# Gate and projection stage: the load of the next sums moved up the DMA queue, and two maxima and one difference moved up VectorE's order

## What is computed

```
out = wave_attention(x)                                  # sampled sums, per token 256 channels
se  = sigmoid(silu(out @ w_se1 + b_se1) @ w_se2 + b_se2) # squeeze, excite
y   = layernorm(x + silu((out * se) @ w_out))
z   = layernorm(y) * ln1_w + ln1_b
q, k, v = split(z @ w_qkv)
y2  = y + softmax(q k^T / 4) v @ w_proj                   # attention, 16 heads
...                                                      # second norm, choice of one of 8 experts, norm
```

## Time and profile before

| | us |
|---|---|
| median of 3 runs | 1665.49 |
| lowest, highest | 1662.57, 1666.0 |
| the profiled execution | 1665.16 |
| its span in the trace | 1663.1 |
| PE busy (93%) | 1542.4 |
| DVE busy (80%) | 1329.3 |
| ACT busy (61%) | 1012.0 |
| busy PE in the gate and projection stage's slices | 8 to 9 tenths |

### The profile page before, as it was taken

The page is one execution under the profiler, slowest core; times in us unless marked ns, Lnnn a source line. Parts: engine busy times, 40 slices in busy tenths (PEclk is TensorE's granted clock), DMA queues, the critical chain, the costliest instruction groups (busy, mean ns, idle before and its releaser), DMA issues. The chain is left out here.

```text
span 1663.1 us, 29306 instructions
## 1 busy us (share of the span) xinstructions
PE 1542.4 (93%) x10078; PEld 838.7 (50%) x10078; DVE 1329.3 (80%) x3006; ACT 1012.0 (61%) x1745; POOL 197.3 (12%) x372
## 2 busy tenths in 40 slices
PE   7588998979988999999999999999998859999997
PEld 6465666655553222222222222222222859999996
DVE  5899999846778888898889888988880756777773
ACT  2699999935445777777777777777776532222221
POOL 3011111131110000000000000000000351222222
PEclk9899999999999999999999999999999978999999
DMA  3300110026956322222232222212302756666661
GB/s 107 89 8 14 49 44 20 22 88 204 264 178 188 77 50 63 71 69 46 61 71 71 52 59 71 71 43 61 70 21 84 237 209 225 208 209 204 204 204 57
DMA packets 159154, 172.22 MB, mean 104 GB/s; under 512 B 72912, under 2 KB 118992, under 8 KB 159008
## 3 DMA queue, kind: packets, MB, share of 16 engines
q1 hardware_dynamic: 153600, 156.60, 32.5%
q0 software_dynamic: 4432, 13.50, 2.1%
q10 hardware_dynamic: 976, 0.24, 0.1%
HBM read 120.73 MB, written 49.23 MB: 102 GB/s over the span
## 5 line engine op out<-in xcount | busy, mean ns | idle before, releaser
L1629 DVE TENSOR_REDUCE at_mx<-at_pmx 128x1 f32<-128x512 f32 x980 | 617.6, 681 | 56.3 <-PE at_pmx L1695 55.4
L1616 ACT ACTIVATE at_p<-at_pst 128x512 f32<-128x512 f32 x1024 | 532.7, 604 | 208.3 <-PE at_pst L1714 208.2
L1695 PE MATMUL at_pmx<-at_k,at_q 96*128 96x512 bf16 x980 | 373.8, 382 | 0.0
L1714 PE MATMUL at_pst<-at_q,at_k 99*128 99x512 bf16 x1024 | 345.7, 379 | 4.7 <-ACT at_p L1616 2.6
L1724 PE MATMUL at_pacc<-at_p,at_v 128*32 128x512 f32 x2048 | 272.7, 604 | 0.9 <-ACT at_p L1616 0.7
L1695 PEld LDWEIGHTS at_pmx<-at_k,at_q 96*128 96x128 bf16 x980 | 95.1, 97 | 238.7 <-DVE at_mx L1629 180.0
L1714 PEld LDWEIGHTS at_pst<-at_q,at_k 99*128 99x128 bf16 x1024 | 98.7, 97 | 156.0 <-ACT at_p L1616 92.8
L873 PE MATMUL ws_pA<-ident,ws_A 128*128 128x128 f32 x1088 | 149.9, 283 | 24.7 <-ACT ws_A L655 22.0
L2226 ACT ACTIVATE ex_hT<-ex_pH 128x1024 f32<-128x1024 f32 x39 | 39.9, 1024 | 204.7 <-PE ex_pH L2281 204.7
L873 PEld LDWEIGHTS ws_pA<-ident,ws_A 128*128 128x128 f32 x1088 | 119.8, 144 | 84.6 <-ACT ws_A L655 39.7
L2241 DVE STREAM_TRANSPOSE ex_zr<-ex_row 32x64 f32<-32x64 f32 x608 | 143.2, 236 | 17.0 <-DMA ex_row<-scratch_routed 8.4
(11 more groups left out here) (271 smaller groups left out, 1568.2 us busy)
## 6 DMA issues: line engine op xcount, KB each, us to landing
ex_w<-in_L_ffn_w SPq DMA_DIRECT2D x39, 1024.0 KB, 5.4
at_q<-scratch_qs SPq DMA_DIRECT2D x192, 64.0 KB, 2.8
at_k<-scratch_ks SPq DMA_DIRECT2D x192, 64.0 KB, 2.9
ex_row<-scratch_routed SPq DMA_DIRECT2D x39, 258.0 KB, 5.0
scratch_v<-gp_v SPq DMA_DIRECT2D x8, 1024.0 KB, 7.9
at_v<-scratch_v SPq DMA_DIRECT2D x32, 256.0 KB, 3.6
w<-in_L_ffn_w SPq DMA_DIRECT2D x16, 512.0 KB, 4.7
scratch_qs<-gp_split SPq DMA_DIRECT2D x16, 384.0 KB, 3.1
```

The lines of the kernel that those rows point to most:

```text
L1616: a.activation(pt[k // 2 % 4][:, k % 2, :], pst[bank(w, k)][:], ACT.Exp).then_inc(exped, 1)
L1629: v.reduce_max(mx[u % 2][:, m // 2, m % 2:m % 2 + 1], pmx[bank(w, m)][:], AX.X).then_inc(red, 1)
L1695: nc.tensor.matmul(pmx[bank(w, m)][:], qst[u][0:ROWS, h, nt * P:(nt + 1) * P], kst[u][0:ROWS, h, kh * HALF:(kh + 1) * HALF], start=True, s ...
L1714: nc.tensor.matmul(pst[bank(w, k)][:], kst[u][:, h, t * P:(t + 1) * P], qst[u][:, h, p * HALF:(p + 1) * HALF], start=True, stop=True).then ...
```

## The change

It has two parts. On SP's queue `load_sums(i + 2)` is issued behind `load_x(i + 1)` and ahead of `load_scores` and of the three stores of chunk i-1, where it stood behind them. On VectorE, after the normalised chunk (L1303), `peaks(i, 5, 6)` and `remain(prev, 2)` go ahead of `low(prev, 0)` and `low(prev, 1)`, and `peaks(i, 6, 7)` goes ahead of `gate_sums(i + 1)`. Nothing is added or removed.

```
 def chunk(i, prev):                       # SP
     if i + 1 < CHUNKS:
         load_x(i + 1)
+    if i + 2 < CHUNKS:
+        load_sums(i + 2)
     if FIRST - 1 <= i < FIRST - 1 + AHEAD:
         load_scores(i - (FIRST - 1))
     if prev is not None:
         for q in range(3):
             store_split(prev, q)
-    if i + 2 < CHUNKS:
-        load_sums(i + 2)
     sp.wait_ge(y0d, i * T + T)
...
                                           # VectorE
+    peaks(i, 5, 6)
     if prev is not None:
+        remain(prev, 2)
         low(prev, 0)
         low(prev, 1)
-        remain(prev, 2)
-    peaks(i, 5, 6)
+    peaks(i, 6, 7)
     if more:
         gate_sums(i + 1)
-    peaks(i, 6, 7)
     if prev is not None:
         remain(prev, 3)
```

## The result

The changed kernel takes 1656.8 us (median of 6 runs, 1655.49 to 1659.32), the kernel before, run beside it, 1666.61 (6 runs, 1662.57 to 1669.06). The ratio is 0.995 with a 95% interval of 0.9933 to 0.9966, that is 5.7 to 11.2 us less. The forecast was 1657.1 us, 8.1 less. The profiled execution took 1656.7 us, its span 1654.9.

A forecast was written before the change was run, and what follows sets the result against it. TensorE was taken to bound the stage, with VectorE near it in chunks with peaks. Gains of 0.6, 0.8, 1.0, 3.3 - 0.3, twice 1.4 and -0.1 sum to 8.1 us: 1665.2 - 8.1 = 1657.1 us, range 1654 to 1662.

The forecast's parts named there:

- chunk 1: TensorE's part 5 waits 0.27 us for the difference and pO 0.31 for the gate; 0.6 gained.
- chunk 2: The squeeze's lost time waiting for the sums' load goes, let through by the earlier gate: 0.8 us gained.
- chunk 3: The squeeze's lost time waiting for the sums' load goes, let through by the earlier gate: 1.0 us gained.
- chunk 4: With no maximum before it, goes from 22.20 to 18.9 us: 3.3 gained, less 0.3 for the scores' loads.
- chunks 5, 6: Sixth and seventh peaks stop waiting (2.2 us), a new stall costs 0.75: 19.6 instead of 21.06, 1.4 gained each.
- the new stall at the first peak: The next chunk's first peak waits 0.75 us for maximum 7, which ends later than TensorE wants it.
- scores' wait: Chunk 4's first peak waits 0.3 us for the scores' loads, with 0 and 3 as ends.
- the squeeze's wait: TensorE's squeeze waits 4 times, 6.5 us counted, for the sums' load; no such wait after the change.
- gate and turn ended together: In chunks 2 and 3 both end together, so the earlier gate lets the load's 0.8 and 1.0 us through.
- its first one: Each microsecond the touched stage ends earlier comes off the total, as later stages get the same work in order.
- only one part works: Rival: something else holds the gate and VectorE's reordering gives nothing; 1 to 3 us gained, 1663 us; chance 0.10.
- The late scores: Rival: chunk 4's first peak waits up to 3 us; 5 us gained, 1660; chance 0.24 with weaker VectorE gain.

The follow-up runs named there:

- e8: The kernel before, unchanged, profiled once more on the chip of the changed kernel's second timing: one time, 1663.88 us.
- e9: The changed kernel, unchanged, timed and profiled again on another chip: 1659.7 us, ratio 0.9964 against the kernel before.
- e1: Changed kernel with VectorE's order put back, so only the sums' load is moved: 1664.96 us, ratio 0.9995 against the kernel before.
- e2: Changed kernel with the sums' load put back, so only VectorE's order is changed: 1661.71 us, ratio 0.9982 against the kernel before.
- e5: Changed kernel with maximum 7 moved right behind difference 3, ahead of two third pieces: 1656.48 us, ratio 0.9925 against the kernel before.
- e4: Changed kernel with difference 2 put back behind the two third pieces, maxima 5 and 6 still moved: 1663.58 us, ratio 0.9992 against the kernel before.
- e3: Changed kernel with maxima 5 and 6 put back, difference 2 still ahead of the third pieces: 1659.26 us, ratio 0.9965 against the kernel before.
- e6: Changed kernel with the sums' load issued behind the scores' loads instead of ahead: 1660.02 us, ratio 0.9951 against the kernel before.
- e10: Changed kernel with maximum 7 right behind difference 3, timed again on the changed kernel's second chip: 1657.61 us, ratio 0.9941 against the kernel before.
- e7: Changed kernel with maximum 5 moved ahead of the norm's last step, before its peak is there: 1664.37 us, ratio 0.9973 against the kernel before.

## Why the prediction was right

Point by point, forecast and measured gain, once from the first traces of before and changed, once from the second (e8, e9):

| term | forecast | first traces | second traces |
|---|---|---|---|
| chunk 1 | 0.6 | 1.39 | 0.71 |
| chunk 2 | 0.8 | 0.94 | 1.07 |
| chunk 3 | 1.0 | 1.11 | 1.10 |
| chunk 4 | 3.3 - 0.3 | 3.16 | 2.74 |
| chunks 5, 6 | 1.4 each | 1.44 each | 1.43, 1.44 |
| chunk 7, to the turn of the maxima | -0.1 | -0.16 | -0.15 |
| stage | 8.1 | 9.45 | 8.5 |
| the new stall at the first peak | 0.75 | 0.73 | 0.73 |
| scores' wait | 0.3 | 0.15 | 0.0 |

The steps held: the squeeze's wait went, chunks 2 and 3 run at TensorE's pace (17.2 forecast), the sixth and seventh peak no longer wait, and the wait for maximum 7 came in their place. e1 and e2 show the point on which the sum hung, that gate and turn ended together in chunks 2 and 3: the sums' load is worth nothing measurable without the earlier gate. e5 shows the new stall by taking it away.

The term that was mis-sized is chunk 1. From its squeeze to chunk 2's pO it is 12.68 us before (374.28 to 386.96) and 11.86 after (374.33 to 386.19), so 0.8 from the change. The prediction added 0.27 and 0.31. The 0.31 was read from starts and holds: from the turn to pO it is 1.19 before and 0.87 after (385.32 to 386.19). The 0.27 was the idle time that the row shows, which is too short where a matmul's printed end is late; by starts it is more: from the squeeze to the turn it is 11.49 before and 10.99 after, so the wait for the difference cost 0.5. The other 0.6 in the first traces is the way to the squeeze at the chunk's start (6.97 and 6.40 us), in which the clock was at its lower level until 370.6 in the one and 370.0 in the other; the second trace of before has 19.03 us for this chunk, so that much is not the change's.

The stage is 9.45 us shorter by the first traces and 8.5 by the second, against 8.1 forecast; the difference lies in chunks 1 and 4, the two whose length differs between the two traces of before. What the total shows is another matter. The first spans fell by 8.2: the stage gave 9.45, what lies behind attention 1.4, attention took 2.0 (from its first to its last score matmul 750.7 us before and 752.6 after), and the stage began 0.6 later. The second spans fell by only 3.5: the stage gave 8.5, what lies behind attention 0.6, attention took 3.1 (751.0 and 754.1), and the stage began 2.5 later. The step of the prediction that does not hold is thus its first one, that each microsecond of the stage comes off the total and nothing behind it gives or takes: attention took 2 to 3 us in these pairs, and other stages vary by as much. The medians fell by 9.8 us in the first comparison (8.3 by the ratio) and by 6.1 in the second. So the terms of the stage are borne out by the traces, while a total within 0.3 us of the forecast is in part luck.

The forecast's own rival, that only one part works, is excluded by e1 to e4. The late scores did not come about: v was issued 2.7 us earlier (405.77 for 408.49) and landed 7.9 us later instead of 8.6. The forecast had 2.2 for the issue and 1.4 for the landing; the two errors cancel to 3.5 for 3.6. And since the landing varies by over a microsecond between executions (8.6 and 8.0 before, 7.9 and 6.7 changed), the split is not a measured effect of the 512 KB moved out of its way.

## What to carry to other kernels

When two engines arrive at a hand-over at the same time, a wait on one of them is worth next to nothing until the other chain is shortened too: read both ends before pricing a wait, and try such edits together, not only one by one. After moving an instruction forward, look at what has become the last one in that engine's round: here the next chunk's first peak waited for it, and moving that last maximum ahead of two independent pieces gave 0.74 us per chunk more. Start-to-start lengths of the chunks of a stage tell such effects to a tenth of a microsecond or better where the total needs many runs for one, as long as the clock is full in them and no transfer sets their length; so look at the clock first, and take a second trace of the same kernel before putting a tenth down to an edit.

## What the runs showed of the hardware

At attention's start TensorE's clock fell to its lower level, 1.2 GHz, in the changed kernel. Windows of the changed kernel after the barrier between the stages (last three columns: clock, DMA share, GB/s):

```profile
514.00:516.00 2.00, 0.10 (x1) 0.13 (x2) 1.28 (x3) 1.26 (x2) 0.00 (x0) 1.00 0.66 252
516.00:518.00 2.00, 2.00 (x8) 0.73 (x7) 1.25 (x3) 1.57 (x3) 0.00 (x0) 0.71 0.97 334
518.00:520.00 2.00, 2.00 (x6) 0.72 (x5) 1.41 (x4) 1.54 (x3) 0.00 (x0) 0.50 0.47 115
520.00:522.00 2.00, 2.00 (x13) 0.44 (x12) 1.38 (x3) 0.74 (x2) 0.00 (x0) 0.94 0.55 145
```

Ahead of the fall TensorE had been nearly idle for 2 us at the barrier. The kernel before has the same idle stretch and no fall in either of its two traces (its mean clock in 524 to 528 us is 1.00 in e8); neither has e3. The other nine traces, e1 with VectorE's old order among them, have it, and attention takes 752.3 to 754.7 us in these nine, 750.7 to 751.0 in the three without. That is 1.3 to 4 us, a good part of what was gained. In e2 and e6 the clock fell once more, 17 us ahead of that (at 503.4 and 500.3 us), right behind the turn of the last maxima, where TensorE had been idle for 1.45 and 0.56 us; this cost 1.7 us of the stage. The changed kernel has the same idle times there and no fall.

The Trainium skill, TensorE: Matmul & The Clock Gate, Part 1, says that the monitor behind the clock runs freely and does not start anew with the kernel, so that the number of slow matmuls at its start differs from run to run. If falls inside a kernel go by the same, it is chance where they strike; no run here tests that.

None in two traces of before against nine in ten of the others leaves open whether the change of timing makes a fall likelier. The clocks of all timed executions lean that way without settling it. On the chip of e8 to e10 the mean clock of a whole execution is 0.9766 over 19 executions of before and 0.9750 over 12 of the changed kernel (standard error of the difference 0.0007); an estimate from these, 0.0016 of 1660 us, is 2.7 us if TensorE was busy in all of it, about what lies between the stage's 8.5 us and the 6.0 us of the total. On the chip of e1 to e4 it is 0.9770 over 34 of before and 0.9752 to 0.9765 in the four variants. On the chip of e5 to e7 it is 0.9755 over 17 of before, and 0.9756, 0.9756 and 0.9745. No experiment here set chance and timing apart.
